# One reduce over two PSUM banks for the score maxima of a fused attention and feed-forward kernel

## The reference

```python
qp = einsum('oc,bcn->bon', Wq, instance_norm(layernorm(x))) + bq
kp = einsum('oc,bcm->bom', Wk, instance_norm(ctx)) + bk
sp = einsum('oc,bcm->bom', Ws, ctx) + bs
attn = softmax(einsum('bcn,bcm->bnm', qp, kp), axis=-1)      # 512 x 512 for each batch
mean = einsum('bnm,bvm->bvn', attn, sp)
std = sqrt(relu(einsum('bnm,bvm->bvn', attn, sp * sp) - mean * mean))
x = x + tanh(g_xattn) * (instance_norm(ctx) * std + mean)
x = x + tanh(g_ffn) * (layernorm(x) @ dequantised(weight_q).T)
```

## Time and profile before

| | |
|---|---|
| median of 3 runs | 201.19 us (200.88 to 202.25) |
| the profiled execution | 201.95 us, of which the span from its first to its last instruction is 200.1 us |
| busy: PE, VectorE, ScalarE, GpSimd | 171.7, 157.0, 127.1, 120.9 us |
| 64 maxima (L669) | 43.5 us busy, 20.3 us of idling before them, 20.2 of it for the scores |
| 64 exponentials (L484) | 44.3 us busy, 33.6 us of idling before them, 30.8 of it for the maxima |
| mean granted TensorE clock | 0.991 of full speed |

### The profile page before, as it was taken

One profiled execution on the slowest core, in us unless ns is written; L12 is line 12 of the kernel. 1 busy time (PEld: TensorE's weight loads), 2 busy tenths in 40 slices (PEclk: granted clock), 3 DMA queues, 4 the chain that ended last, 5 costly groups with the idle time before them and its releaser, 6 DMA issues.

```text
span 200.1 us, 2899 instructions
## 1 busy us (share of the span) xinstructions
PE 171.7 (86%) x816; PEld 106.3 (53%) x816; DVE 157.0 (78%) x337; ACT 127.1 (64%) x271; POOL 120.9 (60%) x143
## 2 busy tenths in 40 slices
PE   0359799999799979997997999799979893999993
PEld 0235556564465545554644565465446442787882
DVE  3868798779778976997699769955978687999751
ACT  2336767947776685959486948676594994563510
POOL 2125578458645754784487458685798957598300
PEclk9999999999999999999999999999999999699999
DMA  6247680773078127804760540073000000011322
GB/s 164 92 102 213 139 233 0 176 217 135 18 166 271 73 66 154 305 5 115 186 227 0 139 126 0 6 179 80 0 2 0 3 0 0 3 52 52 126 87 105
DMA packets 10880, 20.09 MB, mean 100 GB/s; under 512 B 1648, under 2 KB 1776, under 8 KB 10864
## 3 DMA queue, kind: packets, MB, share of 16 engines
q1 hardware_dynamic: 10864, 19.90, 35.3%
HBM read 9.67 MB, written 2.10 MB: 59 GB/s over the span
## 4 chain that ended last, share of the span: by engine, by line
PE 45%; DVE 26%; ACT 12%; issue 7%; DMA 3%; POOL 2%; SPq 2%; ACTq 0%; DVEq 0%
PE pv_bank L361 11%; PE score_bank L337 8%; ACT probs L484 6%; DVE neg_max L669 5%; PE turn_bank L348 5%; PE score_bank L438 4%; PE score_bank L439 4%; DVE VAR L693 4%; PE score_bank L442 4%; PE proj_bank L373 3%; DVE CTX L650 3%; DVE VAR L698 2%; ACT VAR L501 2%; DMA params_sb<-in_params 2%; DVE q_lo L663 2%
## 5 line engine op out<-in xcount | busy, mean ns | idle before, releaser
L886 POOL TENSOR_SCALAR probs<-probs,rden 128x512 f32<-128x512 f32 x64 | 56.4, 882 | 35.0 <-DVE rden L675 34.6
L484 ACT ACTIVATE probs<-score_bank,neg_max 128x512 f32<-128x512 f32 x64 | 44.3, 692 | 33.6 <-DVE neg_max L669 30.8
L361 PE MATMUL pv_bank<-probs_t,values 128*128 128x512 f32 x120 | 60.3, 604 | 0.9 <-ACT VAR L501 0.6
L669 DVE TENSOR_REDUCE neg_max<-score_bank 128x1 f32<-128x512 f32 x64 | 43.5, 681 | 20.3 <-PE score_bank L337 20.2
L348 PEld LDWEIGHTS turn_bank<-ident,probs 128*128 128x128 f32 x256 | 29.7, 142 | 26.7 <-issue 18.0
L348 PE MATMUL turn_bank<-ident,probs 128*128 128x128 f32 x256 | 37.6, 279 | 3.2 <-ACT probs_t L492 2.8
L492 ACT COPY probs_t<-turn_bank 128x512 f32<-128x512 f32 x64 | 37.3, 586 | 0.2
L361 PEld LDWEIGHTS pv_bank<-probs_t,values 128*128 128x128 f32 x120 | 19.7, 190 | 13.0 <-issue 12.5
L337 PE MATMUL score_bank<-k_hi,q_hi 64*128 64x512 f32 x32 | 16.6, 518 | 2.6 <-DVE k_lo_swapped L759 2.5
L337 PE MATMUL score_bank<-k_hi_swapped,q_hi_swapped 64*128 64x512 f32 x32 | 16.6, 518 | 0.0
L438 PE MATMUL score_bank<-w_hi,yt_hi 128*128 128x512 f32 x32 | 14.1, 440 | 0.0
(11 more groups left out here) (106 smaller groups left out, 343.1 us busy)
## 6 DMA issues: line engine op xcount, KB each, us to landing
X<-in_x SPq DMA_DIRECT2D x8, 256.0 KB, 3.1
CTX<-in_context SPq DMA_DIRECT2D x8, 256.0 KB, 3.4
q_hi_swapped<-q_hi SPq DMA_DIRECT2D x16, 128.0 KB, 2.3
q_lo_swapped<-q_lo SPq DMA_DIRECT2D x16, 128.0 KB, 2.4
ctx_now<-in_context SPq DMA_DIRECT2D x8, 256.0 KB, 2.6
sz<-in_scales_zeros SPq DMA_DIRECT2D x4, 512.0 KB, 4.9
out<-result SPq DMA_DIRECT2D x8, 256.0 KB, 2.0
k_hi_swapped<-k_hi SPq DMA_DIRECT2D x15, 128.0 KB, 2.4
```

The lines of the kernel that those rows point to most:

```text
L361: mm = pe.matmul(sums_bank(t, b)[:, :], values[:, i, b, :, :].rearrange("p a c -> p (a c)"), probs_t[b][:, i, :], start=(i == 0), stop=(i ...
L484: act.activation(probs[c % SBANKS][:, :], score_bank[c % SBANKS][:, :], ACT.Exp, bias=neg_max[:, c:c + 1], accum_out=den[:, c:c + 1]).then ...
L669: dve.tensor_reduce(neg_max[:, c:c + 1], score_bank[c % SBANKS][:, :], AX_X, ALU.max, negate=True).then_inc(max_done, 1)
L886: pool.tensor_scalar(probs[c % SBANKS][:, :], probs[c % SBANKS][:, :], rden[:, c:c + 1], 1.0, ALU.mult, ALU.mult).then_inc(probs_done, 1)
```

## The change

The four score banks become two tensors of two neighbouring banks each, `score_pair`; `score_bank` is now a list of views into them, so that all other steps stay as they are. One reduce takes both chunks of a pair and writes two columns of `neg_max`; it counts two on `max_done`, at its end. On VectorE it stands at odd places only, where the even chunk's maximum stood; the odd chunk's maximum, which stood one place later, is gone from there. Before the first tile's loop both pairs are reduced ahead of the first two reciprocals. Lines below the change move by two (L669 becomes L671, L675 becomes L677).

```diff
-        score_bank = [bank(f"score_bank{i}") for i in range(SBANKS)]
+        score_pair = [ctx.enter_context(nc.psum_tensor(f"score_pair{i}", [P, 2, 512], F32))
+                      for i in range(SBANKS // 2)]
+        score_bank = [score_pair[i // 2][:, i % 2, :] for i in range(SBANKS)]
...
-            def maximum(t, c):
-
-                dve.wait_ge(scores_done, CHUNKS * t + 2 * (c // 2) + 2)
-                dve.tensor_reduce(neg_max[:, c:c + 1], score_bank[c % SBANKS][:, :], AX_X, ALU.max,
-                                  negate=True).then_inc(max_done, 1)
+            def maxima(t, c):
+
+                dve.wait_ge(scores_done, CHUNKS * t + c + 2)
+                dve.tensor_reduce(neg_max[:, c:c + 2], score_pair[c // 2 % 2][:, :, :], AX_X, ALU.max,
+                                  negate=True).then_inc(max_done, 2)
...
-            for c in range(AHEAD_S):
-                maximum(0, c)
-                if c > 0:
-                    reciprocal(0, c - 1)
+            maxima(0, 0)
+            maxima(0, 2)
+            for c in range(AHEAD_E):
+                reciprocal(0, c)
             normalise(1, 1)
...
                 for c in range(CHUNKS):
-                    if c + AHEAD_S < CHUNKS:
-                        maximum(t, c + AHEAD_S)
-                    elif has_next(t):
-                        maximum(t + 1, c + AHEAD_S - CHUNKS)
+                    if c % 2 == 1 and c + AHEAD_S < CHUNKS:
+                        maxima(t, c + AHEAD_S)
+                    elif c % 2 == 1 and has_next(t):
+                        maxima(t + 1, c + AHEAD_S - CHUNKS)
```

## The result

The changed kernel takes 208.47 us (median of 4 runs, 208.05 to 208.81) against 201.23 us (4 runs, 200.88 to 202.25): ratio 1.034, 95% interval 1.031 to 1.038. It is slower, by 7.2 us between the medians. Its profiled execution took 208.13 us with a span of 206.3, so 6.2 us more than the profiled execution of before.

What follows compares the result with a forecast made beforehand. PE was taken as nearly full, 17.4 of 18.8 us a tile, idling for VectorE's q_lo. Start and tile 0 to 1 1.3, loops 3.55, tile 6 to 7 0.8, end 0.54: 6.2 us over the 201.19 median, 207.4 (203.7 to 210.3).

Steps and rivals of the forecast that it cites:

- Price of the reduce: VectorE's reduce over two chunks: 1.22 us, low end 1.21, high end 1.38; the next instruction starts 1.14 after.
- Rival C: The long reduce on VectorE has no saving and takes 1.38 us: 210 us in total; chance 0.1.
- Step 1: ScalarE in the loop: exponential of chunk 6 late by 0.53 us and, with no gap behind it, that of chunk 7 too.
- Step 2: VectorE waits for chunk 6's exponential: its reciprocal late by 0.47 us, the reciprocal of chunk 7 late by 0.80.
- Step 3: VectorE before the subtraction: chunk 1's 0.60 us maximum gone, mostly hidden under GpSimd's x_lo; gain 0.1 us, ends 0 and 0.6.
- Rival B: Little change: subtraction and c_hi get ahead of GpSimd, 0.6 us a tile returns, free start; likely 203.5 us; chance 0.17.
- Step 4: After c_hi on VectorE: the longer pair 2/3 costs nothing, covered by GpSimd's c_lo; without cover 0.54 us.
- Step 5: Loop's end: q_lo late by 0.71 us, and with it PE's k projection and the next tile's scores of chunks 6 and 7.
- a sign of being wrong: PE's wait for q_lo gone, with the scores waiting for something else; expected instead was growth from 1.36 to about 2.1 us.
- start, up to T0 of tile 0: Until tile 0's scores of chunks 6 and 7: first reciprocal behind two pairs, 0.5 us counted of 0.74.
- tile 0 to 1: Stretch from tile 0 to 1: PE has only 0.24 us idle, so chunk 7's reciprocal delay of 0.80 shows in full.
- five loops: Five steady middle tiles, each longer by q_lo's delay of 0.71 us: 3.55 us in all.

Runs made afterwards that it cites:

- two_late: Changed kernel's order with two single reduces per pair instead of one, both chunks released by the second: 210.29 us, ratio 1.043.
- two_early: Changed kernel's order with two single reduces per pair instead of one, each releasing its chunk when it ends: 204.28 us, ratio 1.013.
- only_67: Kernel before the change, with only the pair of chunks 6 and 7 taken by one reduce: 206.88 us, ratio 1.026.
- split_67: Changed kernel, with only pair 6/7 of tiles 0 to 6 as two reduces that release one by one: 204.97 us, ratio 1.015.
- max1_late: Kernel before, all maxima single, the next tile's chunk 1 maximum moved behind the subtraction VAR from tile 1 on: 200.07 us, ratio 0.992.
- changed_again: Changed kernel run again without an edit, with the full clock in the first 30 us: 208.63 us in its one run.
- two_early_old_end: two_early, with the last tile's maxima of chunks 6 and 7 back in their old places: 203.94 us, ratio 1.010.
- only_23_45: Kernel before, with only pairs 2/3 (tiles 1 to 7) and 4/5 (all tiles) taken by one reduce each: 202.92 us, ratio 1.007.
- max1_late_23_45: max1_late with pairs 2/3 and 4/5 joined as well: 201.80 us, ratio 0.996 against the kernel before.

## Why the prediction came out as it did

The direction and the cause were right: the loop is lengthened by the late release of chunk 6 (two_late against two_early, only_67, split_67), not by the instruction's own length. Step by step:

- **Price of the reduce,** 1.22 us: 1.217 measured, the next instruction 1.14 behind its start. Rival C is out.
- **Step 1,** 0.53 for the exponentials of chunks 6 and 7: 1.26 instead of 0.73 behind T0, and 3.74 instead of 3.28. That is 0.53 and 0.46.
- **Step 2,** reciprocal of chunk 6 at T0 + 2.07: 2.07. Reciprocal of chunk 7 late by 0.80: 0.83. two_early splits it into 0.53 for the release and 0.30 for the order.
- **Step 3,** a gain of 0.1: this term was mis-sized, it is 0.38. What failed is that the maximum's 0.60 us "lay under that hold". That the order of the two waits leaves the sum unchanged was nearly right: from VAR to the pair 2/3 it is 3.16 instead of 2.97 us. But without the maximum VAR starts 0.57 us sooner behind the reciprocal of chunk 7, gets in front, and now x_lo waits; 0.57 - 0.19 = 0.38 stay. max1_late shows this move alone, -0.35 us a loop. Rival B had it with 0.6, and about two thirds of that came; CTX did last longer (1.51 us), as was said against B.
- **Step 4,** nothing for pair 2/3 under c_lo: from its start to q_lo it is 1.64 us in both kernels (69.86 to 71.50, and 72.89 to 74.53).
- **Step 5:** q_lo late by 0.45 after T0 instead of 0.71, and T0 of the next tile by 0.52. That q_lo's delay carries over was right; that PE's wait for it would grow to 2.1 us was wrong. PE also waits 0.58 for the copied sums and 0.60 for x_lo, on the way to the k projection, so that the wait there shrank to 0.71. It didn't vanish, which the prediction had named as a sign of being wrong. The 0.53 of late sums was put "inside" PE's idling, where it did stay; but x_lo, which now starts behind the subtraction, was not followed to PE.

The sum, term by term, in us:

| term | predicted | measured | how |
|---|---|---|---|
| start, up to T0 of tile 0 | 0.5 | 1.7 | 26.42 - 14.59 against 25.56 - 15.42, from the first reduce |
| tile 0 to 1 | 0.8 | 1.19 | 17.62 - 16.43 |
| five loops | 3.55 | 2.63 | (140.79 - 44.04) - (136.11 - 41.99) |
| tile 6 to 7 | 0.8 | 1.07 | 18.57 - 17.50 |
| after the last T0 | 0.54 | 0.45 | 46.94 - 46.49 |
| sum | 6.2 | 7.0 | |

Between the two profiled executions the difference is 6.2 and not 7.0, because the first reduce of the changed one began 0.83 us earlier (14.59 against 15.42). In changed_again, the same kernel, it began at 15.11, so most of this is scatter. The medians differ by 7.24 us, near the sum from the first reduce on. So the forecast of 207.4, 1.1 us below the median, agreed with the profiled difference by luck, through errors that cancel: the loops were put 0.9 too high, the start 1.2 and the stretches from tile 0 to 1 and 6 to 7 together 0.7 too low. At the start the term for the order was right (0.5 against 0.47 in two_early), but step 1 was not applied there: the release held up the first exponentials as well, and that made T0 of tile 0 another 1.11 us later. From tile 0 to 1 two_early takes 17.07 us, so 0.64 of the 1.19 are the order's and 0.55 the release's. Between tiles 6 and 7, where two_early loses nothing (17.52), PE idles for 1.69 us (at 153.80) for a chunk's probabilities, where it idled 1.16 before the same turns (at 148.11).

On the rule that was weighed: the Trainium skill (Perfetto Trace Analysis, Optimizing Scalar/DVE Operations) says that breaking instructions up may let work finish sooner where the engine isn't saturated but causes bubbles on others. The traces agree: with pair 6/7 alone broken up again the loop went from 19.34 to 18.70 us, though VectorE has one more instruction in it. The same section gives some 125 ns as VectorE's overhead for one operation on PSUM; in VectorE's queue the runs show 0.06 us saved a pair.

Open are the 1.6 us between the median and the profiled execution of two_early_old_end, and why the clock falls in some executions at the start and between tiles 6 and 7.

## What to carry to other kernels

Joining two instructions saves the fixed part of one (0.06 us here) but releases the first result only with the second (0.53 us late); look up who waits for the first half, and join only pairs whose halves find slack, as three of the four here did in the loop, and ask it again of the stretches outside the loop. VectorE, which has idle time in every loop, gained at most 0.1 us a loop here from doing less work, and 0.6 from delivering the awaited result sooner. Where two engines hold one another, try which of them goes first: moving one reduce from in front of a subtraction to behind it was worth more (-0.35 us a loop) than all that the joined instructions save.

## What the hardware showed that was not expected

- Of VectorE's and GpSimd's elementwise operations these held each other, and the order decided which one: the subtraction VAR takes 1.68 us when x_lo is in front of it and 0.98 when it is itself in front, and x_lo then takes 1.71 instead of 1.27. A reduce that reads PSUM ran beside x_lo in max1_late in its usual 0.68 us, and x_lo took 1.71 with it as without. So the place for such a reduce was behind the subtraction.
- A reduce over two neighbouring PSUM banks showed no extra time at the border: 1.217 us for 1024 columns, against 0.681 for 512. The second bank added 0.536 us, about the 0.528 that 512 columns cost when the 0.153 of a 128x1 operation is taken off.
- The granted clock fell to 0.54 (its two levels are 2.4 and 1.2 GHz) in the only_23_45 trace after PE had idled for 1.69 us. In the changed kernel PE idled for as long, for the same probabilities at 153.80, and the clock from there to 157.0 stayed at 1.00. Of the seven traces with 1.69 to 1.75 us of idling there it fell in three (only_23_45, max1_late_23_45, two_late), of the six with 1.16 or 1.17 in none. So the idling alone does not tell when it falls.
